# One eight-layer kernel with two lanes: a new order of the lanes' steps on each engine

## What is computed

```python
x = x + _L0_attn_ref(_layernorm(x), ...)   # a0: causal attention, 16 heads of 8
x = x + _L0_ffn_ref(_layernorm(x), ...)    # f0: 8 experts, 2 chosen per token
x = x + _L1_attn_ref(_layernorm(x), ...)   # a1: linear attention with relu features
x = x + _L1_ffn_ref(_layernorm(x), ...)    # f1: shared branch and 1 of 16 experts
x = x + _L2_attn_ref(_layernorm(x), ...)   # a2: banded attention in blocks of 256
x = x + _L2_ffn_ref(_layernorm(x), ...)    # f2: 32 experts of 64, 4 gates kept
x = x + _L3_attn_ref(_layernorm(x), ...)   # a3: conv, selective state scan, gated mlp
x = x + _L3_ffn_ref(_layernorm(x), ...)    # f3: squared relu, then spike counts
```

## Time and profile before

| what | us |
|---|---|
| median of 3 runs | 2117.89 (2117.66 to 2123.4) |
| the profiled execution | 2106.99 |
| its span, first to last instruction | 2105.2 |
| granted TensorE clock, mean of the span | 0.883 of full speed |
| busy: PE, DVE, ACT, POOL | 1642.7, 1371.6, 909.8, 799.0 |

### The profile page before, as it was taken

The page is one execution under the profiler, slowest core; times in us unless marked ns, Lnnn a source line. Parts: engine busy times, 40 slices in busy tenths (PEclk is TensorE's granted clock), DMA queues, the critical chain, the costliest instruction groups (busy, mean ns, idle before and its releaser), DMA issues.

```text
span 2105.2 us, 28567 instructions
## 1 busy us (share of the span) xinstructions
PE 1642.7 (78%) x10505; PEld 944.0 (45%) x10546; DVE 1371.6 (65%) x3084; ACT 909.8 (43%) x1592; POOL 799.0 (38%) x670
## 2 busy tenths in 40 slices
PE   6797698667878778876768788779768887688667
PEld 3455565112555566423335566524315455564114
DVE  4664355999554455787985435488896544467996
ACT  3462233554435333544535352344544542335553
POOL 2411101995222121373652221165571421025892
PEclk9999898777989899888889998979879998899788
DMA  6005301410000341202100312220210023302210
GB/s 197 1 1 158 99 2 35 135 41 9 13 0 1 99 129 31 85 21 64 52 1 11 99 31 61 74 93 9 85 31 6 1 59 93 98 10 85 75 52 11
DMA packets 96589, 113.66 MB, mean 54 GB/s; under 512 B 7616, under 2 KB 70848, under 8 KB 96192
## 3 DMA queue, kind: packets, MB, share of 16 engines
q1 hardware_dynamic: 94400, 107.63, 17.1%
q0 software_dynamic: 2048, 4.20, 0.7%
HBM read 88.86 MB, written 22.94 MB: 53 GB/s over the span
## 4 chain that ended last, share of the span: by engine, by line
PE 46%; DVE 19%; POOL 9%; ACT 8%; issue 7%; DMA 6%; SPq 6%; DVEq 0%; ACTq 0%; POOLq 0%
PE P L228 9%; POOL M L2079 6%; DVE M L2009 6%; PE P L1634 4%; PE P L1842 3%; SPq L1457 3%; PE P L1217 2%; SPq L1458 2%; DMA W<-in_e 2%; PE P L962 2%; PE P L2137 1%; PE P L390 1%; DMA M<-du 1%; PE P L1222 1%; PE P L217 1%
## 5 line engine op out<-in xcount | busy, mean ns | idle before, releaser
L2009 DVE TENSOR_TENSOR_SCAN M<-P,M 128x512 f32<-128x512 f32 x384 | 446.5, 1204 | 30.2 <-POOL M L2079 18.8
L1842 PE MATMUL P<-M,wt 32*32 32x512 f32 x3072 | 272.4, 780 | 144.7 <-DVE M L2009 108.4
L1923 ACT ACTIVATE P<-M,negA 128x512 f32<-128x512 f32 x384 | 264.2, 690 | 228.9 <-DVE M L2009 213.9
L228 PEld LDWEIGHTS P<-wt,M 128*128 128x128 f32 x2176 | 275.7, 193 | 97.1 <-issue 34.6
L228 PE MATMUL P<-wt,M 128*128 128x128 f32 x2176 | 289.8, 279 | 15.0 <-ACT M L1930 3.4
L2079 POOL TENSOR_TENSOR M<-M 128x512 f32<-128x512 f32 x192 | 244.0, 1305 | 138.0 <-DMA M<-du 76.1
L2079 POOL TENSOR_TENSOR M<-W,M 128x512 f32<-128x512 f32 x192 | 242.3, 1297 | 56.7 <-PE P L1842 56.5
L1842 PEld LDWEIGHTS P<-M,wt 32*32 32x32 f32 x3072 | 40.1, 117 | 330.3 <-DVE M L2009 259.0
L209 POOL TENSOR_TENSOR st<-st,wt 128x4 f32<-128x4 f32 x64 | 84.7, 1323 | 255.9 <-DVE st L192 255.5
L1731 DVE TENSOR_TENSOR M<-M,P 128x512 f32<-128x512 f32 x128 | 87.4, 683 | 93.0 <-PE P L1642 64.5
L1634 PE MATMUL P<-M,wt 128*128 128x512 f32 x256 | 138.0, 623 | 11.0 <-ACT M L1683 6.2
(11 more groups left out here) (338 smaller groups left out, 3236.0 us busy)
## 6 DMA issues: line engine op xcount, KB each, us to landing
W<-in_e SPq DMA_DIRECT2D x152, 192.0 KB
M<-dt SPq DMA_DIRECT2D x64, 256.0 KB, 5.2
M<-xs SPq DMA_DIRECT2D x32, 256.0 KB, 4.2
ys<-M SPq DMA_DIRECT2D x32, 256.0 KB, 2.3
M<-du SPq DMA_DIRECT2D x32, 256.0 KB, 4.9
W<-du SPq DMA_DIRECT2D x32, 256.0 KB, 6.0
W<-xh SPq DMA_DIRECT2D x16, 256.0 KB
xs<-zero SPq DMA_DIRECT2D x2, 1216.0 KB, 10.7
```

Source lines behind the costliest of these rows:

```text
L228: m = e.matmul(out[:, tok(j)], h[:, tok(j)], wgt, start=first and j == 0, stop=last, skip_group_check=True)
L1842: m = e.matmul(t["sums"][i // 2][to:to + 32, :], part("WC", c)[r, r], scan[r, :], start=c == 0, stop=c == 5, tile_position=(32 * i, to))
L1923: e.activation(t["aa"][n % 2][:, :], t["dtr"][i][:, :], EXP, scale=negA[:, c:c + 1]).then_inc(ACT.s, ACT.mark(b, "a3", "aa", n))
L2009: e.tensor_tensor_scan(bb[:, :], t["aa"][n % 2][:, :], bb[:, :], 0.0, MUL, ADD).then_inc(DVE.s, DVE.mark(b, "a3", "scan", n))
```

## The change

No instruction is added or taken away. The five tables `TURNS` (for SP only its first digits) are replaced: between the lanes the steps take a new order by the rule that the first lane goes first where both could go, unless the second has waited long. Waits, tiles and counts of steps are the same. The first line of two of the tables:

```diff
             "tensor": (2179,
-                "000000000807abffc9a7effff50fe100000048e80f2dfffcf3dd9e6d0a3ce7987fc3c3fc03c007ad00f200f32440002dffff"
...
+                "43340909d9b1018856bff0d3bfea10000810844805ebff0c787fce9cb1331bf0e2fffc03c1e03a00000003de000ba1fac7ff"
...
             "sync": (191,
-                "430cfc3a03fcc027fc003edfc00ffc003ffc801ff8007ffa"),
+                "4027fc003ffcc00ffc003ffcc017fc003ffc801ff8007ffa"),
```

More of the change, by code:

```diff
@@ L2242, in program @@
-                "ffff03d501b1be8005c41b6ffc16f7fffd07f2000000112190be18e8fffcc37a31bd19e7f0ffe1e1e0f01d000000f3c01e40"
-                "1fe1b7b3ffffebbbdd1e0398013ff2fffff08f8503dfe"),
+                "43340909d9b1018856bff0d3bfea10000810844805ebff0c787fce9cb1331bf0e2fffc03c1e03a00000003de000ba1fac7ff"
+                "ffc7777ff743cb30080bc1ac292afffe100f3200f66e4003dafe1fd5f7fffd07f40000001121307e18e8fff03bee30fc387f"
+                "8eff861e0f01e03900000079e1a91fc2bbe7fffdddddef1e3e020043fe1561492ffe100f3200f66e4003d5fe173bfffb43f2"
@@ L2244, in program @@
+                "0f230100000978f793ddefccf03bd88787e1f0fff843d0c24e8000003cf06a401fe164ffffffbbbbaf0796606005f0b77090"
+                "afff03d901b1be8009c416dfff8537fffd07f20000001121307e18e8fff03bee30fc387f9cffc21e0f01e0388000001e7807"
+                "a1fac7ffffcee3fff723cb3000bfff8ffff08f8503dfe"),
             "scalar": (1516,
-                "0000010f3ccfb3fb4fb00084900dfff7dbdc9691e38fc0b05b6316d07ffc006b3e8051c0060611983bff57fb4697c1c7aaa0"
-                "02ee98e7fed2a192801094fde6febee44712fe039c2c000fec00fa492953e000000008ffc01fff5959cc1a519adeee26c7ee"
@@ L2247, in program @@
-                "00063084cfec7f6857c471fffdccfda4b2156e38fc007f5010aa012aa924a905ff8ef4b55ffffffffc2c7fc0014cd9fc67fb"
-                "1f600104900ecefebe9378a71f7039c3401fa67d40a75492400800254fc05fffffeffffff1c01ff"),
+                "4363900017cff61366e08224000dfe9bf777223897f01ce1a003f86e841ea904954004254fc053bff4ffb95aafffc0380e7e"
+                "00f79ee67fb1fc00204900ecefcfd91f88e5e81ce1c3803f9fa8166a92490080aafc14c037ffff6bfbd155f00e039f803de0"
+                "3ff7b38499280212bf79f7cfd911c47e82e526805f99f5007d524900020aa7e014f9dff6dfffb4697c2c7fc0014cdfb467fb"
@@ L2249, in program @@
+                "1f600104900ecefcfd91f88e9e81ce1c3402fdba107aa8882d0010953f014ffffffff7fff1c01ff"),
             "vector": (2319,
[L2250 to L2253, removed]
@@ L2254, in program @@
-                "9a5f5d740ff0017fffffffffff578c0be87bf480ffff9330b78000030a1fa80ee7ffdbdf3ed2405000028910f5ff3ffebffc"
-                "81b0280a02805f579e7e901ab75308bd29264beaa4a00281eaa01ffffff3affffff86d5501ffe07e"),
+                "405f41a481ffc00000d81a155006d102f7f5ffca3fc0c02040108405fff3ff5ffcfe050060281401be87ba00157a1ffc03e8"
+                "124c9697d2a95407aa804ceaab7aad057fffffaaa0368747907ffff87a06ff800000a159f80ee7fff3fb3d4ac05000022830"
+                "e7febff5fffa09406028050c0beaf797d403755c527a9249abeaa8aa01fe0060067ffeaab7aad057ffea80568747907ffff8"
@@ L2256, in program @@
+                "7606fc4c0000000177f3eb7df7fffbe840a028880020fff5fcfff5fe0560180600303f55dd7d901ab752217d492152bd548a"
+                "a03d5401f0ceaabbeaff682dffea940be87bf480ffff92b1fa000002851af80ee7ffdbdf3d4ac05000022830e7febff5fffc"
+                "098060280a0c06fabb502d5a1ffc03e88832564beaa95407aa801ffffffffe75fff86d5502ffe07e"),
             "gpsimd": (618,
-                "03f0c3f07c9c3c0007800e0010ce67ff3ffdff8cfc06fc1f0c3000000000000e5ffe9f3fffff6fce1f07f87c302200000000"
-                "03cbfffffffffff8cfc30fc1f0f00000324000000ffffffffffff34"),
+                "4b30e1f07c328000000c900009fff77fdfffff83fc30fc1e8e800003204001803fffff7efdffe0ff00ff07c3c00000908100"
@@ L2259, in program @@
+                "03e1fff3ffffdff8cfc30fc1f0d20000003240000ffffffffffff34"),
             "sync": (191,
-                "430cfc3a03fcc027fc003edfc00ffc003ffc801ff8007ffa"),
+                "4027fc003ffcc00ffc003ffcc017fc003ffc801ff8007ffa"),
         }
```

3 lines of the change are left out of this document (removed).

## The result

The new order is slower: 2138.88 us in the median of seven runs (2125.78 to 2144.66) against 2121.8 of the old order beside it, a ratio of 1.0075 with a 95% interval of 1.005 to 1.0099. A second measurement gave 1.0051 (1.0027 to 1.0076). The forecast of 2106.9 us was faster by half a per cent. The measured time lies inside its range, near its upper end, on the side of rival A. The profiled execution has a span of 2142.6 us. It took 2144.66 us, the longest of the seven, and the old order's profiled execution, 2106.99 us, is shorter than all seven runs beside it (2117.66 to 2123.4). So the two profiles lie 37.4 us apart where the loss is 11 to 17 us: their counts and single instructions can be compared, but a difference of whole pieces between them is too large.

The account below looks back on a forecast made before the run. No engine is full, so which lane stages lie side by side sets the time. Terms -11.4, -4.6 and +5.0 sum to -11.0 us: span 2094.2 for 2105.2, median 2106.9 us, range 2076 to 2145.

Parts of the forecast that it names:

- rival A: Close lanes are slower: the two middle pairs cost 32.4 us more, time 2150 us; chance 0.26.
- The middle, -11.4 us: Batches 2 to 5, lanes kept close: two pairs in 1031.6 us against 1043.0, 11.4 us less.
- 494.7 us of the last pair: Old trace from 1565.2 to the end of batch 7's scans, taken as a middle pair's time without lane 0's tail.
- 16.1 for lane 1's scans with the tail: Lane 0's rest of a3 and f3 among lane 1's scans: 78.6 us in place of 62.5, 16.1 more.
- The 5 for the clock: a0 to a1 took 137.8 or 147.8 us at different clocks; the mean adds 5 us per middle pair.
- lane 0's scans, 81.1 us forecast: Lane 0's 48 scans of a3 without the other lane's scans among them, as in batch 6: 81.1 us.
- the head before them, 33.5 forecast: From the end of lane 0's f2 to its first scan: 33.5 us, as in the old last pair.
- The first pair, -4.6: Batches 0 and 1, scans no longer mixed and an earlier start: 517.6 us against 522.2, 4.6 us less.
- The last pair, +5: Batches 6 and 7, nearly the same order, but its a0 to a1 had the good clock: 5 us more.
- B: Clock and sum of work decide; all terms shrink, time stays within 6 us of 2117.9; chance 0.20.
- C: Lane 0's tail is free beside lane 1's scans: 44 us less, 2063; chance 0.12 with steps towards it.
- the mark of 90 for rival A: In the changed profile, lane 1's scans of batches 1, 3 and 5 taking 90 us or more would show rival A.

Follow-up runs that it names:

- the repeat: The whole new order, unchanged, timed a second time against the old order, on the same chip as the pieces: 1.0051, median 2128.29 us.
- the new middle alone: New order only from lane 0's f3 end in batch 0 to that in batch 4, old order before and behind, against the old order: 1.0065.
- the ends alone: Old order in the middle, new order for batches 0, 1, 6 and 7, against the old order: 0.9956, median 2106.28 us.
- filler products: Two zero-adding PE products after 20 of lane 1's 24 gathers per batch; against the old order, 1.004 in the new order and 1.0012 in the old.
- the new middle without the stretched multiplications: New order in the middle only, with the 64 multiplications of a3's norms moved from DVE to ACT, against the old order: 0.9992.

## Why the prediction was wrong, point by point

**The start.** That no engine is full and that the lanes' company sets the time holds. But "an order can only fill or open gaps" was the false premise: the new order made instructions longer, by 18.1 us on DVE.

**The middle, -11.4 us, is the step that failed.** It came out at +31.0 in the profiled execution, +13.7 in the repeat (1056.7) and +18.4 with the new middle alone (1061.4). The pair's 515.8 us was put together from 494.7 us of the last pair plus 16.1 for lane 1's scans with the tail plus 5. The 16.1 was right: 78.6 us forecast, 80.3 and 76.7 measured. The 5 for the clock was right: a0 to a1 took 146.6, 142.9 and 144.1 where I had 142.8. The term that was mis-sized is hidden in the 494.7: **lane 0's scans, 81.1 us forecast, 90.8 and 91.9 measured**, together with the head before them, 33.5 forecast, 37.7 and 36.3 measured. By the profiled execution the two pairs took 538.3 and 535.7 us, 42.4 more than the 1031.6 forecast. Lane 0's scans alone are 20.5 of these and the heads 7.0; a0 to a1 adds 3.9, f0 to f2 6.6 (180.9 and 184.5 us against 179.4), and the rest of the pairs 4.4. I had carried the scans over from the old last pair, where one of the norms' multiplications among them is stretched; in the new middle four are, each by some 1.0 us, and without them the scans are 3 to 4 us shorter. The row itself was no accident: in five other kernels with the old order at the end it takes 80.8 to 85.6 us. In eleven traces with the new order at the end the same 48 scans of batch 6 take 86.5 to 91.3 us. It was the company that differs, though I had called it the same.

The cause of the loss against the old order is shown: 16 multiplications of 0.28 us stand 1.3 us each beside POOL's products, and without them the new middle's 0.65% is gone (0.9992). Why the new middle does not reach the forecast even so is open. What is left in that trace, 1046.5 - 1031.6 = 14.9 us, is as much as lane 0's scans in that kernel (87.1 and 90.0 us) are above 81.1. No experiment here isolates its cause.

**The first pair, -4.6.** The profiled execution has 518.8 against 522.2, -3.4. Batch 0's f2 ended at 311.8 (I had 317.9, less 2 for the start) and its head took 36.5 us (42); its scans took 88.5 (81.1) and from their end to the end of lane 1's it was 81.5 (78.6). Against the forecast that is 9.6 us won and 10.3 lost, so the nearness of 518.8 to 517.6 is luck: the errors cancelled. **The last pair, +5.** It came out at 549.8 against 540.0, +9.8, at the upper bound. But the ends alone, timed, are 0.44% faster, 9.3 us, where these two terms give about nothing. In their trace the first piece is 509.9 us and the last 540.3. In the other traces without filler products the first piece takes 505.6 to 518.8 us in the new order and 518.2 to 524.4 in the old. So the first pair's gain was put too small. The early norm of lane 1, answering in the timeline of DVE after,

```profile
7.22 0.84 DVE L184 BATCH_NORM_STATS2 st<-xt 128x6 f32<-128x128 f32 x4
```

starts at 7.22 us and no longer at 28.48; the unmixed scans of the earlier trace rows lie in that piece as well. They were not tried apart.

**The rivals.** A named the right sign and nearly the size (2150 with all pairs like the first loop; intervals of 538.3 and 535.7 us where it would have 532), and it was right that the loss lies beside the scans. Its mechanism was wrong: it put the loss into lane 1's scans, from 21.8 us above 62.5, and from the end of lane 0's scans to the end of lane 1's it stayed at 78.5 on the mean. Its other half, a0 to f2 of both lanes meeting on PE, is at most 6.0 of the middle's 31.0 us. B, a time within 6 us of the old one, did not come: the loss is 17 us by the medians and 11 in the repeat. That the clock is its main cause is not borne out by the filler products. C, the tail for nothing, did not occur.

**The marks.** "Batch 1's first scan comes after batch 0's last but a few" and "POOL under 70" came true in batch 0 (67.4 of 88.5 us); "79 to 84 us" for batch 0's scans failed, and was the mark of the term that was mis-sized. Lane 0's f3 ended at 518.8, 1057.1 and 1592.8, not near 518, 1034 and 1549. "Lane 1's scans take 75 to 82 us" failed by its letter: 85.1, 93.8 and 88.2 us. In batches 3 and 5 they begin 13.5 and 11.5 us before lane 0's end, which my sum of one after the other had not, and the rest is 80.3 and 76.7; so the mark of 90 for rival A told nothing. "Intervals near 530 mean that close lanes are slower as such" was a false inference: the intervals came and more, and the new middle without the stretched multiplications is not slower than the old one.

**The outcome.** Two versions beat both kernels of the case: the old middle with the new ends, 0.9956, and the new order with the multiplications on ACT, 0.9968. Their intervals overlap.

## What to carry to other kernels

When a stretch is carried over from another place of the trace, compare the durations of the same instructions in both, not only their sum: here an instruction with a median of 0.28 and a longest of 1.30 us had a neighbour on another engine that it waited for, and the order decided how often they met. Before short DVE instructions are placed into a dense stretch of POOL work, look up in the trace which kinds are stretched there, and give those to ACT, or place them elsewhere. Such a move pays only where they meet: in the old order it gave nothing.
